# Value products of four heads at a time in the second layer, keys projected already transposed, rope in one product

## What is computed

```
# first layer, 16 heads, three attentions over one query
nq = rms(x @ w_cq) * g_qnorm                       # 96 wide
q = concat(nq @ w_dq_nope, rope(nq @ w_dq_rope))   # 32 + 64 a head
ckv = rms(x @ w_ckv) * g_kvnorm                    # 32 wide
k1 = concat(ckv @ w_dk_nope, rope(x @ w_krope / 16))   # 32 a head, + 64 that all heads share
v1 = ckv @ w_dv                                    # 32 a head
ks, vs = from the 64 tokens of highest score x @ w_imp
kw, vw = rope(x @ w_wink), x @ w_winv
out = g0*attn(q,k1,v1,causal) + g1*attn(q,ks,vs) + g2*attn(q,kw,vw,causal)
x = x + out @ w_proj
x = x + spikes(relu(ln(x) @ W_fc.T)**2 @ W_proj.T)
# second layer, 16 heads of 16
q, k, v = split(ln(x) @ W_qkv.T); q, k = rope(q), rope(k)
x = x + attn(q, k, v, causal) @ W_o.T
x = x + ln(x) @ sign(weight).T
```

## Times and profile before

| | us |
|---|---|
| median of 3 runs | 3159.23 |
| lowest, highest | 3157.82, 3160.17 |
| the profiled execution | 3157.54 |
| its span, first to last instruction | 3155.8 |

### The profile page before, as it was taken

How to read it: one execution, slowest core, us unless ns; L and a number is a source line. 1 busy time by engine, 2 the same in 40 slices (tenths; PEclk the granted TensorE clock), 3 DMA queues, 4 the chain that set the end, 5 groups by cost and what they waited for, 6 DMA issues and landing times. The chain is left out here.

```text
span 3155.8 us, 56164 instructions
## 1 busy us (share of the span) xinstructions
PE 2975.5 (94%) x19216; PEld 2139.5 (68%) x19216; DVE 1960.8 (62%) x6610; ACT 1470.0 (47%) x3276; POOL 1010.1 (32%) x1828
## 2 busy tenths in 40 slices
PE   4999999989999999999999999999999999999977
PEld 3776776657766677666777667776677767776654
DVE  3666656665566655766566765667566675565654
ACT  1545344454445544455444554445444554445433
POOL 0233232332334223333233332333223332333221
PEclk8999999999999999999999999999999999999999
DMA  3011001100110001100101001110011000110000
GB/s 117 28 30 31 26 25 32 31 13 21 39 38 24 23 31 31 32 18 24 36 25 39 17 26 33 35 30 12 28 38 32 25 16 24 32 32 17 13 8 28
DMA packets 58858, 91.54 MB, mean 29 GB/s; under 512 B 19920, under 2 KB 32976, under 8 KB 58320
## 3 DMA queue, kind: packets, MB, share of 16 engines
q1 hardware_dynamic: 58576, 87.95, 9.6%
HBM read 81.61 MB, written 5.24 MB: 28 GB/s over the span
## 5 line engine op out<-in xcount | busy, mean ns | idle before, releaser
L1735 ACT ACTIVATE PR<-work 128x512 f32<-128x512 f32 (+1 forms) x1088 | 643.5, 598 | 766.4 <-PE work L1104 614.0
L1356 DVE CUSTOM_DVE_ANT_0 work<-work,KEEPB 128x128 f32<-128x128 f32 (+3 forms) x1536 | 665.4, 476 | 102.0 <-PE work L1065 101.0
L1853 POOL TENSOR_SCALAR_AFFINE_SELECT PR<-PR 128x256 f32<-128x256 f32 (+1 forms) x960 | 366.7, 386 | 798.4 <-ACT PR L1735 792.0
L1337 DVE TENSOR_TENSOR BIG<-work,BIG 96x512 fp32r<-96x512 f32 (+1 forms) x448 | 276.1, 626 | 366.7 <-ACT BIG L1632 360.7
L1065 PE MATMUL work<-BIG 96*128 96x448 f32 (+8 forms) x1664 | 453.8, 364 | 38.7 <-DVE NMX L1356 22.8
L1102 PE MATMUL work<-BIG 99*128 99x512 f32 (+4 forms) x1152 | 422.3, 367 | 9.7 <-DVE X L1510 4.4
L1065 PEld LDWEIGHTS work<-BIG 96*128 96x128 f32 (+1 forms) x1664 | 277.2, 196 | 197.4 <-issue 81.5
L1146 PE MATMUL outs<-PR,ONES 128*32 128x512 f32 (+4 forms) x2304 | 406.5, 460 | 0.0
L1843 POOL TENSOR_TENSOR TOK<-AB 128x256 f32<-128x256 f32 (+1 forms) x320 | 215.2, 673 | 593.1 <-DVE AB L1307 561.2
L1103 PE MATMUL work<-BIG 96*128 96x512 f32 (+4 forms) x1152 | 383.4, 333 | 0.0
L1104 PE MATMUL work<-BIG 96*128 96x512 f32 (+4 forms) x1152 | 381.2, 331 | 0.0
(11 more groups left out here) (166 smaller groups left out, 4843.6 us busy)
## 6 DMA issues: line engine op xcount, KB each, us to landing
NRM<-park SPq DMA_DIRECT2D x112, 192.0 KB, 3.1
WKW<-w_kw_dram SPq DMA_DIRECT2D x64, 256.0 KB, 2.7
WSEL<-w_sel_dram SPq DMA_DIRECT2D x64, 256.0 KB, 3.0
R<-park SPq DMA_DIRECT2D x72, 64.0 KB, 2.0
HN<-x_dram SPq DMA_DIRECT2D x8, 512.0 KB, 5.0
X<-x_dram SPq DMA_DIRECT2D x8, 512.0 KB, 3.9
out_dram<-X SPq DMA_DIRECT2D x7, 512.0 KB, 3.3
R<-park SPq DMA_DIRECT2D x16, 192.0 KB, 3.0
```

The costliest lines, as they stand in the source:

```text
L1337: read_work(v.tensor_tensor(dst[1], src, dst[0].bitcast(F32), ALU.subtract), use)
L1356: last = v.tensor_tensor_reduce(ps[:, lo:hi], ps[:, lo:hi], KEEPB[:, T - (hi - lo):T], -1.0, -NEG, ALU.add, ALU.min, dst)
L1735: a.activation(PR[0:rows, j % NP, :], ps[0:rows, :], ACT.Exp).then_inc(exp_ready, 1)
L1853: gp.affine_select(blocks, blocks, [[0, len(cols)], [1, P]], ALU.is_ge, 0.0, base=0, channel_multiplier=-1).then_inc(exp_masked, 1)
```

## The change

**Groups of four heads.** In layer 1 the units of two pairs are interleaved by the list `QUAD`, and `values_of_heads` multiplies for four heads in one call: three calls for two pairs in place of three for one. The maxima of both pairs of a group are now due in the period before it, the odd pair's 3.2 units after the even one's.

**Keys.** Of `nv`, the nope keys are now one product for a pair and all 512 tokens, with the weights as stationary (`nope`); the result is already transposed, so that ACT and DVE write it directly into `K1`. The rotated keys are transposed from `KR` by `rotated_keys`, once for each parity of `K1` and sequence, and written for both heads by one instruction of ACT and one of DVE. The values of two pairs come from one piece (`val`) at every even pair. `TOK` holds only the five pieces that are rotated.

**Rope.** DVE multiplies with cosines and sines in one instruction of 512 columns, and POOL adds the halves, one of them read in reverse. One of the four copies per tile out of the transposed heads of layer 1 moves from DVE to ACT. The due times in all tables are moved a little.

```diff
-PV = [[(2 * k, 2 * k + 1) for k in range(6)], [(0, 1), (2, 3), (4,)]]
-NPV = [len(k) for k in PV]
+PV = [(2 * k, 2 * k + 1) for k in range(6)]
+NPV = len(PV)
+QUAD = [(0, 0), (0, 1), (1, 0), (1, 1), (0, 2), (0, 3), (1, 2), (1, 3), (0, 4), (1, 4)]
+QUAD_PV = [QUAD[0:4], QUAD[4:8], QUAD[8:10]]
+PRODUCTS = [NPAIR * NPV, NPAIR // 2 * len(QUAD_PV)]
...
-PIECES = [("qk", 0), ("qk", 1), ("nv", 0), ("qk", 2), ("qk", 3), ("nv", 1), ("sel", 0)]
+PIECES = [("qk", 0), ("qk", 1), ("nope", 0), ("qk", 2), ("qk", 3), ("val", 0), ("sel", 0)]
...
-AFTER = [dict(pv=2.67, recip=1.8, scale=3.2, late_recip=2.48, late_scale=5.5, scale_gap=0.82, last_recip=1.9, last_scale=3.81, piece=-2.58, gap=0.66, piece_tr=2.15, max=4.98, max_gap=0.31, mt=1.78, rows=-5.38),
-         dict(pv=3.17, recip=2.64, scale=5.15, last_recip=0.53, last_scale=4.91, max=-0.21, max_gap=1.03, mt=2.68, piece=32.73, gap=1.08, piece_tr=1.63)]
+ROPED = [m for m in range(NPIECE) if PIECES[m][0] in ("qk", "sel")]
+NROPED = len(ROPED)
+def pieces_of(p):
+    return [m for m in range(NPIECE) if p % 2 == 0 or PIECES[m][0] != "val"]
+def tok_number(g, m):
+    return NROPED * g + ROPED.index(m)
+def piece_before(g, m, n):
+    k = tok_number(g, m) - n
+    return (k // NROPED, ROPED[k % NROPED]) if k >= 0 else None
+AFTER = [dict(pv=2.67, recip=1.97, scale=3.42, late_recip=2.37, late_scale=5.46, scale_gap=0.91, last_recip=1.73, last_scale=3.91, piece=-2.58, gap=0.66, piece_tr=1.99, max=4.98, max_gap=0.31, mt=1.97, rows=-5.38, kr=0.44, val=3.0),
+         dict(odd=3.2, pv=3.12, recip=2.71, scale=5.16, last_recip=2.0, last_scale=4.22, max=-0.18, max_gap=1.03, mt=2.45, piece=32.73, gap=1.08, piece_tr=1.44, kr=37.93, val=-0.0)]
...
+    for q in range(NPAIR // 2 if layer else 0):
+        for k, (p, i) in enumerate(QUAD):
+            at += [(2 * n * q + k, ("unit", 2 * q + p, i)), (2 * n * q + k + 1.2, ("mask", 2 * q + p, i))]
+        for k, units in enumerate(QUAD_PV):
+            t = 2 * n * q + QUAD.index(units[-1]) + o["pv"]
+            at.append((t, ("pv", q, k)))
+        output(t, q, 0, True)
...
+        b = n * (p - 1) if layer == 0 else 2 * n * (p // 2 - 1) + o["odd"] * (p % 2)
...
-                elif what == "nv":
-                    for tt in range(2):
-                        t2 = 2 * t + tt
-                        last = mm(ps[:, tt * P:(tt + 1) * P], CKVT[:, t2 * P:(t2 + 1) * P],
-                                  WQ[:, w * P:(w + 1) * P], start=True, stop=True)
+                elif what == "nope":
+                    last = mm(ps[:, :], WQ[:, 64 * w:64 * w + P], CKVT[:, :], start=True, stop=True)
+                elif what == "val":
+                    for t in range(NT):
+                        last = mm(ps[:, t * P:(t + 1) * P], CKVT[:, t * P:(t + 1) * P],
+                                  WQ[:, 512 + 64 * w:512 + 64 * w + P], start=True, stop=True)
...
+            def rotated_keys(use):
+                _, n, _ = use
+                pe.wait_ge(kr_ready, n + 1)
+                ps, done = take(use, W)
+                for t in range(NT):
+                    last = nc.tensor.transpose(ps[0:ROPE, t * P:(t + 1) * P], KR[:, t, :], ID[:, :])
...
-                            elif layer == 1:
-                                v = VP[:, j, 2 * p + h, :]
...
+            def values_of_heads(s, q, k):
+                units = QUAD_PV[k]
+                pe.wait_ge(exp_masked, MASK0[1, s] + len(QUAD) * q + QUAD.index(units[-1]) + 1)
+                if k == 0:
+                    pe.wait_ge(evacuated, OUT0[1, s] + max(q - 2, 0))
+                    if q == 0:
+                        for i in range(2):
+                            was_read(pe, work, work_read, ("v", s, i))
+                parts = [(p, i, part) for p, i in units for part in UNITS[1][i]]
+                parts.sort(key=lambda x: (x[2][2], x[0], x[2][1]))
+                for p, i, (_, h, j, col) in parts:
+                    row = 64 * p + 32 * h
+                    slot = unit_number(s, 1, 2 * q + p, i) % NP
+                    last = mm(OB[q % 3][row:row + 32, j * P:T], VP[:, j, 4 * q + 2 * p + h, :],
+                              PR[:, slot, col:col + T - j * P], start=(j == 0), stop=(j == 2), skip_group_check=True)
...
+                if what == "nope":
+                    use, par = ("piece", g, m), g % 2
+                    ps = full(dve, use, WORK)
+                    k, _, _, r, _ = work.of[use]
+                    dve.wait_ge(work_read[k], r - 2)
+                    for h in range(2):
+                        hi, lo = (K1[par][n][ROPE:D0, h, KEEP:] for n in range(2))
+                        read_work(v.tensor_tensor(lo, ps[32 * h:32 * h + 32, :], hi.bitcast(F32), ALU.subtract), use)
...
+            def low_rotated(use):
+                k, _, _, r, _ = work.of[use]
+                ps = full(dve, use, WORK)
+                dve.wait_ge(work_read[k], r - 1)
+                hi, lo = (K1[use[2]][n][0:ROPE, :, KEEP:] for n in range(2))
+                both = ps[0:ROPE, :].unsqueeze(1).broadcast_to([ROPE, 2, T])
+                read_work(v.tensor_tensor(lo, both, hi.bitcast(F32), ALU.subtract), use)
...
-                src = src.rearrange("p h (j d) -> p h j d", j=2)
-                cos = COS0[0:rows, t:t + 1, :].unsqueeze(1).broadcast_to([rows, heads, 2, 32])
-                sin = SIN0[0:rows, t:t + 1, :].rearrange("p a (j d) -> p a j d", j=2).broadcast_to([rows, heads, 2, 32])
-                one, two = rope_products(src, cos, sin, a4, b4)
-                read_work(one, ("piece", g, m))
-                read_work(two, ("piece", g, m))
+                shape = [rows, 2, heads, ROPE]
+                read_work(v.tensor_tensor(rotations(i, rows, heads), src.unsqueeze(1).broadcast_to(shape),
+                                          ROPE0[0:rows, t, :, :].unsqueeze(2).broadcast_to(shape), ALU.mult),
+                          ("piece", g, m))
...
-                for k in range(1, 4):
+                for k in (1, 3):
...
+                        read_work(copy(K1[g % 2][0][ROPE:D0, h, KEEP:], ps[32 * h:32 * h + 32, :]), use)
+                    return
+                if what == "val":
+                    p, n = g % NPAIR, g // NPAIR
+                    if p >= 2:
+                        act.wait_ge(pv_done, PV0[0, n] + NPV * (p - 1))
+                    for k in range(2):
+                        read_work(copy(VV[:, (p + k) % 3, :, A1, :],
+                                       ps[:, :].rearrange("p (t n) -> p t n", t=NT)[:, :, 64 * k:64 * k + 64]), use)
...
+                use = ("heads", n, t, 2)
+                ps = full(act, use, WORK)[:, :].rearrange("p (g k) -> p g k", g=4)
+                read_work(copy(KB[:, 0:4, t * P:(t + 1) * P], ps), use)
...
-                if what == "nv":
-                    gp.tensor_copy(dst.rearrange("p (t h) d -> p t h d", t=2),
-                                   KR[:, 2 * t:2 * t + 2, :].unsqueeze(2).broadcast_to([P, 2, 2, ROPE])).then_inc(tok_ready, 1)
-                    return
...
-                a4, b4 = ab(g * len(ROPED) + ROPED.index(m), rows, heads, 32)
-                merge = "p h j d -> p h (j d)"
-                gp.tensor_tensor(dst, a4.rearrange(merge), b4.rearrange(merge), ALU.add).then_inc(tok_ready, 1)
+                a4, b4 = (rotations(i, rows, heads)[:, n, :, :].rearrange("p h (j d) -> p h j d", j=2) for n in range(2))
+                gp.tensor_tensor(dst.rearrange("p h (j d) -> p h j d", j=2), a4, b4[:, :, ::-1, :],
+                                 ALU.add).then_inc(tok_ready, 1)
```

314 lines of the change are left out of this document (165 added, 149 removed), and 8 rows, old and new, of tables (MID_A, MID_C).

## The result

| | us |
|---|---|
| median of 4 runs | 3106.93 |
| lowest, highest | 3102.25, 3114.26 |
| the kernel before beside it, median of 4 runs | 3158.70 |
| ratio, with its 95% interval | 0.9836 (0.9822 to 0.9849) |
| the profiled execution, its span | 3114.26, 3112.4 |

The change makes the kernel 52 us faster (43 from profiled to profiled execution). The forecast was 3074, 84 us faster by its own sum; the time is 1 us outside its range. On two later occasions the same kernel took 3111.8 and 3109.0 us; its gain is 47 to 52 us.

The account below looks back on a forecast made before the run. PE was taken as the bound in both layers. Profiled execution 3157.5 - 84 (value calls) - 17 (pieces) - 4 (`VV` waits) + 21 (new layer 1 waits) = 3073.5 us; forecast 3074, range 3047 to 3106.

Parts of the forecast that it names:

- a group of four heads should cost 2.53 us where it costs 5.06: Value products of layer 1: four heads in one call cost what two cost, 81 us less over 32 groups.
- the 0.03 a call that I added for the hold-up: Value calls of layer 1: each call also holds up its predecessor, so halving 192 calls saves 3 us more.
- The rival that four products don't run together: Layer 1 value products reading four different slots do not overlap; the 81 us stay away, 3125 to 3155 us, chance 0.05.
- nothing of that counts: Layer 0 pieces: less work for DVE, ACT and POOL, at 64%, 46% and 33%, gains nothing, except waits on ACT's copies.
- this sign: Layer 0 passes no shorter, instead of 317 to about 314.5 us, would show the forecast wrong.
- 17 us for fewer instructions and 4 for waits on `VV`: Layer 0 pieces: PE saves 0.27 us a pair, 17 us; half its 8.1 us wait behind ACT's `VV` copies, 4 us.
- The named cost for the rotated keys: Layer 0 pieces: an eighth of 8 transposes of `KR`, 0.10 us a pair on PE.
- Allowed 0.6 us a pass: Start of a layer 1 pass: the first unit now stands behind the maxima of both pairs, 0.6 us given back each pass.
- more of the maxima already done: Start of a layer 1 pass: the first unit moves from 2176.53 to about 2178.6, with more maxima done by then.
- the first rival: Layer 1 becomes bound by reading out, up to 69 us given back instead of 21: 3098 to 3122 us, chance 0.14.
- the slower rival: Layer 1 value calls each wait for their last unit's exponential and mask, 95 us or twice that; chance 0.03.
- better than all bounds: The case of a time under 3050 us, chance 0.07; shortest time by the bounds was 3045.

Follow-up runs that it names:

- the edits on `val` and on the rotated keys: Two kernels against the changed one: `val` due at 35.5 instead of 38.13, 3105.03 us; rotated keys copied for one head only from the third sequence, 3106.24 us.
- The corners: Neither part, four-head groups, new pieces, both, as us from the kernel before: old due-time tables 0, -34, +36, -1; new tables +13, -42, +13, -50.
- undoing the due time: Changed kernel with the maxima of the second pair of each layer 1 pass due where they stood before: 3099.11 us, against 3111.8 in the same job.
- cheap maxima: Layer 1 maxima taken over the last 128 columns of each segment only: 3060.94 us in the changed kernel, 3127.00 us in the kernel before.
- the fill: Changed kernel with 4 and 7 unused products of 512 columns ahead of the first two waits on maxima in each layer 1 pass: 3108.92 us.

## Why the forecast missed

**Right: what PE executes.** The step "a group of four heads should cost 2.53 us where it costs 5.06" holds to 0.02 us a call. Over one sequence the value products fell by 10.03 us (10.5 with the 0.03 a call that I added for the hold-up, which the sum doesn't show) and the pieces' instructions by 1.92 (2.1). The rival that four products don't run together is out, and so is the rule of "TensorE: Matmul & The Clock Gate" (Part 3) of the Trainium skill on overlapping weight loads, by which a load waits for running products of its own row group and the saving would have been up to 31 us smaller: with eight and sixteen instructions on the same row group in a call, it isn't.

**Wrong: "nothing of that counts" for the pieces.** The prediction had named this sign itself: a pass of layer 0 no shorter, "which would mean that `nope` and `val` stand where PE waits for a bank". It is 318.7 us before and after, and they do wait. The forecast took 17 us for fewer instructions and 4 for waits on `VV`, since DVE, ACT and POOL had less to do. With the tables held new, the pieces bring 0 to 8 us, not 21. PE's instructions for them did get 1.92 us of a sequence cheaper, 15 us in eight. The named cost for the rotated keys was 0.10 us a pair for PE; what stands behind it are 1.01 us on ACT and 1.22 on DVE for one bank, and new waits for readers at `nope`, `val` and `KR`. PE's idle time of a sequence rises from 2.0 to 3.5 us in the 9 us ahead of the first unit, from 4.0 to 5.1 within the pass of layer 1, and from 6.4 to 8.9 in the rest. The rest is 6.6 with the groups and the new tables alone, so 2.3 us of it come with the pieces, against 1.92 us of work saved. That the two readings in series are what costs this is argued from the rows: the edits on `val` and on the rotated keys moved the waits and gave at most 3 to 5 us in five sequences. Over five steady sequences the pieces bring nothing (1878.1 and 1878.4 us).

**Wrong: the tables had no term.** "The due times in all tables are moved a little" stood in the description of the change, and the forecast priced each part as if it could be taken out of its order. The corners show that the order is worth 49 us to the changed kernel (-1 to -50) and costs the old one 13. The first is layer 0's: with both parts the old tables make the stretch between passes of layer 1 6.9 us longer in each sequence (325.6 and 318.7). The second is the pass of layer 1 (61.8 and 65.6), where calls for two heads wait for masks on POOL. In terms of the forecast: tables +13 (0), groups -55 (-63), pieces -8 (-21); sum -50 (-84). This way of dividing is one of several, since the parts don't add across tables; by the old tables it would read -34 for the groups, +33 for the pieces and -49 for the tables.

**Too small: the start of a pass.** Allowed 0.6 us a pass; undoing the due time gives 1.6 us a pass back (12.7 in 8), and the first unit comes 2.6 us later after the first product of maxima (9.20 and 6.56). The place was nearly right: the forecast's 2178.6 is 7.8 us after the first reading at 2170.76, and it is 8.6 now. The credit for "more of the maxima already done" was too large: DVE reads all of both pairs ahead of the first unit, and PE stands still for a part of it.

**Partly right: the first rival.** Layer 1 bound by reading out would give 3098 to 3122, and the time is 3107. DVE's reading carries 14 to 19 us of its 24 to 48, but not where the rival put it: within the pass, cheap maxima gave the changed kernel no more than the one before. The difference stands at the start (3.8 and 1.8 us), so these 14 to 19 us and the 12.7 of the due time are probably for the most part the same; both edits together were not run. "TensorEngine Tiling" (Performance Considerations, PSUM bottleneck) of the Trainium skill says that tiling speeds up TensorE and not the reading of PSUM, which may then be the bottleneck. That holds here to this extent: PE's instructions got cheaper and DVE's reading of the banks did not. But reading held up PE before as well: less reading alone made the kernel before 32 us faster, with DVE busy for 66% of a pass of layer 1. A share of busy time far below one didn't show it.

**Not it: the slower rival.** Value calls of the groups wait 2.7 us in all for masks, not 95. The clock is a small part: about 40 us more are run at 1.2 GHz between 100 and 3000 us (75 before, 115 after), which can account for most of the 2.2 us a sequence by which maxima and units got slower from start to start. Keeping it at its higher level at the start of the passes brought 1.1 to 1.5 us of a sequence, net of the fill, and 3 us of the whole.

**Left open.** With cheap maxima the change is worth 66 us, with the expected work of PE saved and 28 us more idle time over five sequences. The readers of the pieces' banks and the order are the candidates; the edits on `val` and the rotated keys moved these waits for little or nothing, and the tables were not tried one at a time, so it is open which due times make the new pieces fit. Nor is it settled which waits of the old tables bring the lower clock that goes with them. (In the prediction, "better than all bounds" starts at 3050 though the bounds give 3045; this had no part in the miss.)

## What to carry to other kernels

When a change comes with a new order, price the order as a part of its own, and measure the corners: each part in the old and in the new order. Where PE waits for banks, an instruction removed from it need not be worth its time; ask for each new piece how long its bank is held by all of its readers in series, and not only how busy these engines are. And test for a bound by cheapening the suspect in both kernels: here the yardstick itself moved by 32 us. Then look at which stretch the difference lies in.

## What the runs showed of the hardware

Eight column-tiled products of 32-bit floats with 32 columns each, recorded as sixteen instructions, take as long from start to start as four (1.00 and 0.99 us for 384 and 128 columns), in four column groups and one row group. A wait of 1 to 2 us of PE at the start of a pass was followed by granted clocks of 0.76 over 11 us; a fill that kept the clock at 1.00 brought the first unit forward by 0.57 of 9.20 us, since another engine paces most of it. A bank read by two engines in series was read for 1.01 us by ACT and, from 0.10 us after that, for 1.22 by DVE (64 x 1024 elements each).
